# Clears beside the gathers removed, and the gathered rows of two graph layers summed as three bf16 terms

## The chip, the cores and the metric

The kernel runs on one core of one Trainium2 chip. The metric is the device time of one execution in microseconds. The time before is the median of three runs, 2423.22 us (2419.51 to 2429.55). A further execution was profiled: 2415.55 us, of which the profile shows a span of 2413.6 us. All rows below come from that execution.

The engines are named as the profile names them: PE is the matrix engine (PEld its weight loads), DVE the vector engine (VectorE), ACT the scalar engine, POOL GpSimd, SP the engine that issues most of the plain DMAs.

## The reference

A graph has 6250 nodes with 128 features and 106250 edges, sorted by their target node. A normalisation with relu is followed by three layers of mean aggregation, then comes a second normalisation and a message layer:

```
sage(h):  agg[v] = sum over edges (u -> v) of h[u] / max(deg[v], 1)
          out    = agg @ W_l.T + b_l + h @ W_r.T
h  = relu(layernorm(x))
h1 = relu(sage1(h));  h2 = relu(sage2(h1)) + h1;  x = x + sage3(h2)
h  = relu(layernorm(x))
msg[e] = silu(concat(h[src[e]], edge_attr[e]) @ mw1 + mb1)
x = x + h + silu(concat(h, sum of msg over edges into v) @ uw1 + ub1) @ uw2 + ub2
```

What costs time is the sum over incoming edges, four times over. In the kernel these passes are l = 0, 1, 2 (the three aggregations) and l = 3 (the messages).

## The kernel before

The edges are cut into 831 tiles of 128. In pass 0 most edges are handled without a gather. VectorE builds two one-hot tiles for each of the first 600 edge tiles, PE multiplies them into a small table of counts (which source node occurs for which target), ACT moves the tables to a staging tile and sends them to DRAM. SP reads them back in pieces, and a dense product of all node rows with these counts gives the sums. The sum goes in rounds of 49 steps, one step for each 128 source nodes (`dense_step`, line 1128). Passes 1 and 2 read the same tables again: 10 rounds, 490 steps. In these, ACT turns six of seven units of 500 counts from fp16 to a rounded fp32 form and VectorE the seventh (`turn_unit`, line 563), and each step is two products of PE with the high and the low half of the node rows (line 1148).

The remaining edges go in blocks of three tiles. POOL gathers the source rows of a tile from a table in DRAM by an indirect DMA (line 847), three for a block. VectorE makes a one-hot tile of the targets (`hot`, line 1578), PE multiplies rows and one-hot into 31 columns (`sum_block`, line 1098 in passes 1 and 2, line 1101 in pass 0), and VectorE adds these columns to the accumulator (`add`, line 1588). Pass 0 has 117 such blocks, passes 1 and 2 have 77 each. In pass 0 the table holds each row as three bf16 parts, so a block is nine bf16 products and three for the degrees. In passes 1 and 2 it holds fp32 rows, and a block is three fp32 products.

The order of the work is written out by hand in ticks. In passes 1 and 2 a tick is one dense step, and block n stands at tick 34 + n*452//77, about every 5.9 ticks (`block_tick`). In pass 0 a tick is one counted tile, and from tick 78 on a block stands at every 4.4 ticks. Each engine runs its own list in that order. Blocks may be gathered ahead: there are seven places (`LAPS`), and POOL waits until the block that had the place has been summed. In pass 2 the columns of finished nodes are closed chunk by chunk beside the steps (`chunk_work`): average, convolution, second normalisation and message rows, for 13 chunks of 512 nodes.

After each gather of passes 0 to 2 POOL also clears a small tile that nobody reads (line 853). Each such clear waits for the one before it, and 813 gathers have one. Pass 3 gathers 759 tiles by the same line, without clears.

## Time and profile before

| what | us |
|---|---|
| median of three runs | 2423.22 |
| profiled execution, and its span | 2415.55, 2413.6 |
| pass 0, first to last gather | 115.61 to 625.28 |
| pass 1, first to last gather | 690.17 to 997.67 |
| pass 2, first to last gather | 1052.02 to 1362.11 |
| pass 3, first to last gather | 1420.83 to 2397.99 |

The span falls into the four passes with their gathers and three stretches between them, in which the sums are averaged, the layer's small products are made and the table for the next pass is written. The profile's chain of waits tells which engine's work set the end. The groups of instructions show the mean time of one and what ended the idle time before it. In the order of time one sees single instructions with their starts, and in brackets how long the engine had been idle. A matrix product's time overlaps its neighbour's, so its pace is read from one start to the next.

### The profile page before, as it was taken

The numbers are of one execution on the slowest core, as the hardware profiler recorded it, in microseconds if no ns is written. First come the engines' busy times: TensorE is split into PE (matmuls) and PEld (weight loads), VectorE is DVE, ScalarE is ACT, GpSimd is POOL, SyncE is SP. The second block draws the span as 40 slices with busy tenths as digits, with TensorE's granted clock in tenths as the row PEclk, the third lists the DMA queues.
The fourth block names the chain that finished last, engine by engine and source line by source line (L and its number), as shares of the span: only waits on it lengthen the run. The fifth ranks groups of instructions, "written<-read, shape, count | busy, mean of one in ns | idle before, by whom it ended". The sixth has DMA issues, their size and how long they took to land.

```text
span 2413.6 us, 45284 instructions
## 1 busy us (share of the span) xinstructions
PE 2083.5 (86%) x13062; PEld 1628.3 (67%) x13062; DVE 1477.5 (61%) x4334; ACT 1136.1 (47%) x2077; POOL 1845.1 (76%) x2479
## 2 busy tenths in 40 slices
PE   1589988988789888899999959989989898988987
PEld 0234544444367677667777748888889888888876
DVE  8878877777633223354444447666767667676664
ACT  4777766666487666587667732111111111111111
POOL 4488888888478888588888537777777777777775
PEclk9689999999899999999999979999999999999997
DMA  4389888878578777668787644434444444444432
GB/s 121 115 284 302 298 284 263 282 260 279 209 232 254 242 239 233 186 201 260 223 246 240 203 146 136 121 108 121 113 120 114 115 122 112 116 117 117 118 108 54
DMA packets 270049, 447.28 MB, mean 185 GB/s; under 512 B 34149, under 2 KB 219816, under 8 KB 263144
## 3 DMA queue, kind: packets, MB, share of 16 engines
q1 hardware_dynamic: 206680, 267.00, 36.3%
q0 software_dynamic: 55920, 114.62, 17.1%
q10 hardware_dynamic: 7200, 62.72, 6.6%
q8 instruction: 109, 1.79, 0.3%
q14 instruction: 140, 1.14, 0.1%
HBM read 363.79 MB, written 80.42 MB: 184 GB/s over the span
## 4 chain that ended last, share of the span: by engine, by line
POOL 61%; issue 15%; PE 13%; DVE 6%; ACT 2%; DMA 2%; DVEq 0%; POOLq 0%; ACTq 0%; SPq 0%
POOL gath L847 55%; PE bank L1148 7%; POOL early_rest L853 6%; PE bank L1098 2%; DMA gath<-table,src_sb 1%; DMA table<-shared 1%; PE bank L1356 0%; ACT shared L973 0%; DVE acc L1867 0%; PE bank L1218 0%; PE bank L1357 0%; ACT unit L563 0%; DVE iota_f L1374 0%; PE bank L1219 0%; PE bank L1156 0%
## 5 line engine op out<-in xcount | busy, mean ns | idle before, releaser
L847 POOL DMA_INDIRECT gath<-table,src_sb x1572 | 1560.2, 992 | 367.5 <-issue 363.7
L1148 PE MATMUL bank<-unit,halves 128*128 128x500 f32 x1960 | 510.2, 407 | 17.7 <-ACT unit L563 12.3
L563 ACT CAST unit<-region 128x500 fp32r<-128x500 f16 x840 | 454.2, 606 | 124.9 <-PE bank L1148 121.9
L1036 ACT ACTIVATE msg<-msg 128x384 f32<-128x384 f32 x277 | 145.2, 524 | 745.6 <-DVE msg L1676 691.4
L1198 PE MATMUL bank<-source_hot,last_halves 128*128 128x384 f32 x2352 | 494.3, 356 | 0.0
L936 ACT CAST shared<-bank 128x490 f32 x600 | 373.7, 623 | 172.6 <-PE bank L1120 140.2
L1148 PEld LDWEIGHTS bank<-unit,halves 128*128 128x128 f32 x1960 | 362.0, 194 | 93.7 <-ACT unit L563 22.4
L1704 DVE TENSOR_SCALAR source_hot<-source_f,source_col 128x384 fp32r<-128x384 f32 x1176 | 421.0, 421 | 0.8 <-PE bank L1198 0.5
L1198 PEld LDWEIGHTS bank<-source_hot,last_halves 128*128 128x128 f32 x2352 | 414.1, 196 | 3.8 <-issue 3.8
L1588 DVE TENSOR_TENSOR acc<-acc,bank 128x31 f32 (+1 forms) x548 | 104.9, 191 | 398.6 <-PE bank L1098 271.7
L1156 PE MATMUL bank<-region,parts 128*128 128x500 f16 x1176 | 321.6, 381 | 9.8 <-DVE dense_sum L1599 9.8
L1098 PEld LDWEIGHTS bank<-onehot,msg 128*128 128x128 f32 x1662 | 229.5, 200 | 145.2 <-ACT msg L1036 139.0
L1098 PE MATMUL bank<-onehot,msg 128*128 128x31 f32 x1662 | 229.5, 275 | 103.7 <-ACT msg L1036 94.1
L1676 DVE TENSOR_TENSOR msg<-bank,gath 128x384 f32<-128x384 f32 x253 | 140.2, 554 | 260.5 <-issue 183.8
L1633 DVE TENSOR_SCALAR region<-iota_h,key 128x540 bf16<-128x540 f16 x600 | 225.0, 409 | 35.0 <-PE bank L1120 32.2
L1183 PE MATMUL bank<-mw,region 128*128 128x128 f32 x1518 | 238.9, 296 | 1.2 <-DVE shared L1751 1.2
L1117 PE MATMUL bank<-region 128*128 128x490 bf16 x600 | 223.2, 400 | 18.8 <-DVE region L1633 13.0
L1183 PEld LDWEIGHTS bank<-mw,region 128*128 128x128 f32 x1518 | 199.5, 200 | 6.6 <-issue 6.6
L853 POOL MEMSET early_rest<- 128x128 bf16 x813 | 186.1, 229 | 0.4
L1098 PEld LDWEIGHTS bank<-onehot,gath 128*128 128x128 f32 x924 | 123.7, 192 | 55.7 <-issue 47.7
L1156 PEld LDWEIGHTS bank<-region,parts 128*128 128x128 bf16 x1176 | 91.6, 101 | 91.8 <-issue 14.8
L1098 PE MATMUL bank<-onehot,gath 128*128 128x31 f32 x924 | 118.9, 265 | 28.9 <-DMA gath<-table,src_sb 28.4
(165 smaller groups left out, 1763.6 us busy)
## 6 DMA issues: line engine op xcount, KB each, us to landing
region<-counts SPq DMA_DIRECT2D x196, 875.0 KB
counts<-shared ACTq DMA_DIRECT2D x50, 1225.0 KB
region<-in_edge_T SPq DMA_DIRECT2D x138, 384.0 KB, 3.3
gath<-table,src_sb POOLq DMA_INDIRECT x1572
table<-shared SPq DMA_DIRECT2D x36, 256.0 KB, 2.3
table<-parts SPq DMA_DIRECT2D x12, 384.0 KB, 2.6
source_row<-in_src_row SPq DMA_DIRECT2D x24, 192.0 KB, 3.7
acc<-in_x SPq DMA_DIRECT2D x12, 256.0 KB, 5.4
```

The source lines that it names most:

```text
L563: copy(units[h][:, :].rearrange("p (b n) -> p b n", b=RG), ring[:, q, :, h * G:(h + 1) * G]).then_inc(done, 1)
L847: pool.indirect_dma_start(out=(gath if l > 0 else gath_parts)[:, BT * place + j, :], out_offset=None, in_=table[l], in_offset=bass.Indirec ...
L853: nc.gpsimd.memset(early_rest[:, :], 0.0).then_inc(early_rested, 1)
L936: counted = nc.scalar.copy(stage[:, g % 2, :, bass.ds(at, CW)], count_bank(t))
L1098: mm = nc.tensor.matmul(summed_in(l, n)[:, 0:W], of, onehot[:, n % HOTS, j, :], start=(j == 0), stop=(j == BT - 1))
L1117: mm = nc.tensor.matmul(count_bank(t), low_of(t), pairhot[:, t % NPAIR, 0:KW].rearrange("p (h w) -> p h w", h=NTILE), start=True, stop=(t ...
L1148: mm = nc.tensor.matmul(sum_bank(ordinal), halves[:, hi, a, :], units[h][:, :], start=(hi == 0 and a == 0), stop=(hi == NTILE - 1 and a == 1))
L1156: mm = nc.tensor.matmul(sum_bank(ordinal)[:, 0:g * G].rearrange("p (b n) -> p b n", b=g), parts[:, hi, a, :], ring[:, q, 0:g, h * G:(h + 1 ...
L1183: mm = nc.tensor.matmul(edge_bank(n)[:, j * D:(j + 1) * D], efT[:, h % NEF, t * P:(t + 1) * P], mw[:, 1, :], start=True, stop=True)
L1198: mm = nc.tensor.matmul(bank[7][:, 0:BT * P], last_halves[:, h, a, :], source_hot[:, y % NHOT, :], start=(h == 0 and a == 0), stop=False)
L1633: nc.vector.tensor_scalar(pairhot[:, t % NPAIR, :], iota_h[:, :], key[:, t:t + 1], None, ALU.is_equal).then_inc(pairhot_ready, 1)
L1704: nc.vector.tensor_scalar(source_hot[:, y % NHOT, :], source_f[:, k % 2], source_col[:, h:h + 1], None, ALU.is_equal).then_inc(source_hot_ ...
```

## The change

The clears go, with their tile and semaphore. In passes 1 and 2 VectorE now prepares each gathered block: it subtracts from the fp32 rows their own upper 16 bits (read in place as a bf16 number), which gives a rest in fp32, and subtracts from the rest the rest's upper 16 bits, which gives a third term, written as bf16. PE then sums a block by nine bf16 products: the upper halves of the rows and of the rest are read in place with a stride of two, the third term is dense. There are two buffers for rest and third term. The two subtractions stand four ticks ahead of the block in VectorE's list. PE's wait for the gather in passes 1 and 2 becomes a wait for the split, and VectorE waits for the gather. The semaphores of a fallback for leftover edges, which does not run here, are shared by two passes each.

```diff
+SPLIT_AHEAD, NSPLIT = 4, 2
+def splits(l, i):
+    return [n for n in range(BLOCKS[l]) if l in (1, 2) and block_tick(l, n) - SPLIT_AHEAD == i]
...
+        def upper(of):
+            return of.rearrange("p t d -> p (t d)").bitcast(BF16).rearrange("p (t d u) -> p t d u", t=BT, u=2)[:, :, :, 1]
...
                             in_offset=bass.IndirectOffsetOnAxis(ap=src_sb[:, t:t + 1].bitcast(U32), axis=0),
                         ).then_inc(gathered[place], 16)
-                        if l < 3:
-                            after(pool, early_rested, BT * (BLOCKS_BEFORE[l] + n) + j)
-                            nc.gpsimd.memset(early_rest[:, :], 0.0).then_inc(early_rested, 1)
...
-                if l < 3:
+                if l == 0:
                     pe.wait_ge(gathered[place], 16 * BT * (fills + 1))
+                elif l < 3:
+                    pe.wait_ge(block_split, done - BLOCKS_BEFORE[1] + 1)
                 for j in range(BT):
                     t = BT * place + j
-                    if l > 0:
-                        of = msg[:, n % NMSG, j, :] if l == 3 else gath[:, t, :]
+                    if l in (1, 2):
+                        for a, of in enumerate([upper(gath[:, BT * place:BT * (place + 1), :]), upper(rest[:, n % NSPLIT]), third[n % NSPLIT][:, :, :]]):
+                            mm = nc.tensor.matmul(summed_in(l, n)[:, 0:W], of[:, j, :], onehot_h[:, n % HOTS, j, :, 1],
+                                                  start=(j == 0 and a == 0), stop=(j == BT - 1 and a == 2))
+                    elif l > 0:
+                        of = msg[:, n % NMSG, j, :]
                         mm = nc.tensor.matmul(summed_in(l, n)[:, 0:W], of, onehot[:, n % HOTS, j, :], start=(j == 0), stop=(j == BT - 1))
...
+                def split(n):
+                    place, fills = slot(l, n)
+                    g = BLOCKS_BEFORE[l] - BLOCKS_BEFORE[1] + n
+                    of = gath[:, BT * place:BT * (place + 1), :]
+                    dve.wait_ge(gathered[place], 16 * BT * (fills + 1))
+                    after(dve, block_summed, BLOCKS_BEFORE[l] + n - NSPLIT + 1)
+                    nc.vector.tensor_tensor(rest[:, n % NSPLIT], of, upper(of), ALU.subtract).then_inc(rest_made, 1)
+                    dve.wait_ge(rest_made, g + 1)
+                    nc.vector.tensor_tensor(third[n % NSPLIT][:, :, :], rest[:, n % NSPLIT], upper(rest[:, n % NSPLIT]), ALU.subtract).then_inc(block_split, 1)
...
                         if n + HOTS < BLOCKS[l]:
                             hot(n + HOTS)
+                    for n in splits(l, i):
+                        split(n)
                     if l > 0 and (i + TURN_AHEAD) % UNITS == BY_DVE and i + TURN_AHEAD < STEPS[l]:
                         turn_unit(dve, nc.vector.tensor_copy, l, i + TURN_AHEAD, units_by_dve)
```

The added lines move the numbers of the lines behind them: the gathers of line 847 are those of line 866 afterwards, the sums of line 1098 are line 1116, and the dense products of line 1148 are line 1170.

On POOL, at the beginning of pass 0, the list stood before as follows (`acc` is the accumulator that is cleared ahead of the pass, `gath` the seven places, `src_sb` the source numbers):

```order
L773 TENSOR_TENSOR parts<-gath,parts 128x128
L821 MEMSET acc 128x6372
L847 DMA gath<-table,src_sb 128x384
L853 MEMSET early_rest 128x128
L847 DMA gath<-table,src_sb 128x384
```

and now:

```order
L785 TENSOR_TENSOR gath<-acc,parts 128x128
L792 TENSOR_TENSOR parts<-gath,parts 128x128
L840 MEMSET acc 128x6372
L866 DMA gath<-table,src_sb 128x384 x351
L821 TENSOR_LOAD left_flag
```

The 351 gathers of the pass follow each other with nothing between them; passes 1 and 2 have 231 each in the same way.

On VectorE, in pass 1 around the first two blocks, the list stood before as follows (`onehot` is made six blocks ahead, `unit3` is the unit of counts that VectorE turns, `first_row` gives the place in the accumulator):

```order
L1588 TENSOR_TENSOR acc<-acc,bank0 128x31
L1578 TENSOR_TENSOR onehot<-iota_f,rel 128x93
L563 CAST unit3_63<-region_58 128x500
L1584 TENSOR_LOAD first_row
L1584 ISA x2
L1588 ISA
L1588 TENSOR_TENSOR acc<-acc,bank1 128x31
```

and now:

```order
L1600 TENSOR_TENSOR onehot<-iota_f,rel 128x93
L582 CAST unit3_63<-region_58 128x500
L1619 TENSOR_TENSOR rest_75<-gath_57 128x384
L1621 TENSOR_TENSOR third1_77<-rest_75 128x384
L1606 TENSOR_LOAD first_row
L1606 ISA x2
L1610 ISA
L1610 TENSOR_TENSOR acc<-acc,bank1 128x31
```

The two subtractions of block 1, with their wait for its gathers, now stand ahead of the addition of block 1, and behind what was queued for block 0.

On PE, in pass 1 at the first block, the list stood before as follows (`unit` is a unit of counts, `halves` the node rows, two products for a step):

```order
L1148 MATMUL bank<-unit_65,halves 128x500 x2
L1098 MATMUL bank<-onehot,gath 128x31 x3
L1148 MATMUL bank<-unit_66,halves 128x500 x2
L1148 MATMUL bank<-unit_60,halves 128x500 x2
L1148 MATMUL bank<-unit_61,halves 128x500 x2
```

and now:

```order
L1170 MATMUL bank<-unit_65,halves 128x500 x2
L1116 MATMUL bank<-onehot,gath 128x31
L1116 MATMUL bank<-onehot,rest 128x31
L1116 MATMUL bank<-onehot,third_76 128x31
L1170 MATMUL bank<-unit_66,halves 128x500 x2
```

Of the nine products of the block only the first three are shown, the other six repeat them for the second and third tile. The place of the block among the steps is the same.

## Rows read from the trace of the kernel before

**Rows 1.** The page's shares of the chain that ended last, by line.

```profile
POOL gath L847 55%; PE bank L1148 7%; POOL early_rest L853 6%; PE bank L1098 2%; DMA gath<-table,src_sb 1%; DMA table<-shared 1%; PE bank L1356 0%; ACT shared L973 0%; DVE acc L1867 0%; PE bank L1218 0%; PE bank L1357 0%; ACT unit L563 0%; DVE iota_f L1374 0%; PE bank L1219 0%; PE bank L1156 0%
```

**Rows 2.** Passes 0, 1, 2: busy us by engine, then clock, DMA share, GB/s.

```profile
115.00:627.00 512.00, 460.49 (x3735) 233.23 (x3736) 388.80 (x1082) 343.94 (x553) 453.64 (x703) 0.96 0.85 279
690.00:1006.00 316.00, 287.15 (x1427) 235.85 (x1428) 93.83 (x310) 225.14 (x415) 270.59 (x462) 0.97 0.79 245
1052.00:1364.00 312.00, 295.50 (x1509) 240.31 (x1508) 131.63 (x427) 229.29 (x443) 273.18 (x462) 0.98 0.81 251
```

**Rows 3.** POOL in order of time, pass 1, then pass 3: start, us, idle before.

```profile
770.50 0.95 POOL L847 DMA_INDIRECT gath<-table,src_sb  x1 [0.16 <-issue]
...
2049.80 0.94 POOL L847 DMA_INDIRECT gath<-table,src_sb  x1 [0.30 <-issue]
```

**Rows 4.** Groups of pass 0, then pass 1: busy, mean ns of one | idle before.

```profile
L847 POOL DMA_INDIRECT gath<-table,src_sb x351 | 370.3, 1055 | 57.7 <-issue 57.5 <-PE bank L1105 0.2
L853 POOL MEMSET early_rest<- 128x128 bf16 x351 | 84.0, 239 | 0.1
...
L847 POOL DMA_INDIRECT gath<-table,src_sb x231 | 220.1, 953 | 38.7 <-issue 38.2 <-PE bank L1098 0.5
L853 POOL MEMSET early_rest<- 128x128 bf16 x231 | 51.0, 221 | 0.1
```

**Rows 5.** PE's waits for gathers, passes 0, 1, 2: us in total, times, longest.

```profile
PE bank L1101 <- DMA gath<-table,src_sb: 32.4, 23, 5.1
...
PE bank L1098 <- DMA gath<-table,src_sb: 27.3, 31, 2.4
...
PE bank L1098 <- DMA gath<-table,src_sb: 1.1, 3, 0.7
```

**Rows 6.** Pass 0 in time: block 0's last gather, block 0 summed, block 42 summed.

```profile
118.82 0.95 POOL L847 DMA_INDIRECT gath<-table,src_sb  x1 [0.16 <-issue]
...
144.94 0.46 PE L1101 MATMUL bank<-onehot,gath 128*128 128x31 bf16 x9
...
308.31 0.38 PE L1101 MATMUL bank<-onehot,gath 128*128 128x31 bf16 x9 [1.03 <-DMA gath<-table,src_sb]
```

**Rows 7.** Pass 2 in time, a gather that begins inside a VectorE instruction.

```profile
1195.90 0.69 DVE L1757 TENSOR_TENSOR acc<-acc,shared 128x512 f32<-128x512 f32 x1
...
1196.14 1.28 POOL L847 DMA_INDIRECT gath<-table,src_sb  x1 [0.17 <-issue]
```

**Rows 8.** Groups of pass 0: VectorE's long instructions with two inputs in SBUF.

```profile
L1628 DVE TENSOR_TENSOR region<-iota_h,low 128x768 bf16<-128x768 f16 x93 | 88.6, 953 | 14.3 <-PE bank L1120 13.8
L1641 DVE TENSOR_TENSOR region<-iota_f,group_rel 128x500 bf16<-128x500 f32 x94 | 59.5, 672 | 11.5 <-PE bank L1167 10.8 <-issue 0.7
```

**Rows 9.** Groups of the whole span: VectorE's fp32 instructions on SBUF.

```profile
L1757 DVE TENSOR_TENSOR acc<-acc,shared 128x512 f32<-128x512 f32 x12 | 8.2, 685 | 1.3 <-ACT shared L973 1.2
L1510 DVE TENSOR_TENSOR region<-region 128x600 f32<-128x600 f32 x1 | 0.8, 784 | 0.0
L1461 DVE TENSOR_TENSOR region<-region 128x600 f32<-128x600 f32 x1 | 1.6, 1616 | 0.0
```

**Rows 10.** PE in time: a block in pass 0, a block and six steps in pass 1.

```profile
561.02 0.40 PE L1101 MATMUL bank<-onehot,gath 128*128 128x31 bf16 x9
561.26 0.23 PE L1105 MATMUL bank<-onehot,ones_h 128*128 128x31 bf16 x3
...
771.03 0.75 PE L1098 MATMUL bank<-onehot,gath 128*128 128x31 f32 x6
771.62 2.97 PE L1148 MATMUL bank<-unit,halves 128*128 128x500 f32 x12
```

**Rows 11.** The chain, last gather of pass 1; in time, last gather and block of pass 2.

```profile
997.67 4.98 DMA gath<-table,src_sb
...
1362.11 0.95 POOL L847 DMA_INDIRECT gath<-table,src_sb  x1 [0.17 <-issue]
...
1383.18 0.75 PE L1098 MATMUL bank<-onehot,gath 128*128 128x31 f32 x6
```

More of the change, by code:

```diff
@@ L164 @@
 LAPS = 7
-EARLY_REST = 128
 FETCH_EVERY, FETCH_FROM, COPY_AFTER, FETCH_LAG = 11, 4, 12, 16
@@ L399, in gnn_kernel @@
         last_halves = over("last_halves", [P, NTILE, 2, D], F32R, halves_at)
+        rest = over("rest", [P, NSPLIT, BT, D], F32, shared_at + 4 * 4 * 2 * CH)
+        third = [over(f"third{q}", [P, BT, D], BF16, at + 2 * UNIT) for q, at in enumerate([tail_at, key_at])]
+        assert 4 * (4 * 2 * CH + NSPLIT * BT * D) <= 2 * SHARED and len(third) == NSPLIT
+        assert tail_at + 2 * UNIT + 2 * BT * D <= key_at and key_at + 2 * UNIT + 2 * BT * D <= shared_at
+        def upper(of):
+            return of.rearrange("p t d -> p (t d)").bitcast(BF16).rearrange("p (t d u) -> p t d u", t=BT, u=2)[:, :, :, 1]
         stats = sb("stats", [P, 2, JC, 6])
@@ L422, in gnn_kernel @@
         fetch_copied = sem("fetch_copied")
+        rest_made = sem("rest_made")
+        block_split = sem("block_split")
         consts_in = sem("consts_in")
@@ L433, in gnn_kernel @@
         onehot_ready = sem("onehot_ready")
-        early_rest = sb("early_rest", [P, EARLY_REST], BF16)
-        early_rested = sem("early_rested")
         block_summed = sem("block_summed")
@@ L475, in gnn_kernel, with left_from @@
         LEFT = ["idx", "gathered", "onehot", "summed", "added"]
-        lf = [{n: sem(f"left{l}_{n}") for n in LEFT + (["ef_in", "edge_mm", "pre", "msg"] if l == 3 else [])} for l in range(4)]
+        left_sems = [{n: sem(f"left{k}_{n}") for n in LEFT + (["ef_in", "edge_mm", "pre", "msg"] if k == 1 else [])} for k in range(2)]
+        lf = [left_sems[l % 2] for l in range(4)]
+        def left_from(l, each):
+            return l // 2 * each
         def apart(eng):
@@ L639, in left_edges @@
                     with sp.Fori(0, NT) as t:
-                        sp.wait_ge(s["added"], NCH * t + 1)
+                        sp.wait_ge(s["added"], NCH * t + 1 + left_from(l, NCH * NT + 1))
                         apart(sp)
@@ L646, in left_edges @@
                             sp.dma_start(ef_left, edge_T[:, bass.ds(t * P, P)]).then_inc(s["ef_in"], 16)
-                    sp.wait_ge(s["added"], NCH * NT + 1)
+                    sp.wait_ge(s["added"], NCH * NT + 1 + left_from(l, NCH * NT + 1))
             def load_last_rows(c):
@@ L805, in left_edges @@
                     with pool.Fori(0, NT) as t:
-                        pool.wait_ge(s["idx"], 16 * t + 16)
+                        pool.wait_ge(s["idx"], 16 * t + 16 + left_from(l, 16 * NT))
                         apart(pool)
@@ L1268, in left_edges @@
                         else:
-                            pe.wait_ge(s["gathered"], 16 * t + 16)
+                            pe.wait_ge(s["gathered"], 16 * t + 16 + left_from(l, 16 * NT))
                         for c in range(NCH):
                             w = min(CH, NP - c * CH)
-                            pe.wait_ge(s["onehot"], NCH * t + c + 1)
+                            pe.wait_ge(s["onehot"], NCH * t + c + 1 + left_from(l, NCH * NT))
                             if l > 0:
@@ L1281, in left_edges @@
                             mm.then_inc(s["summed"], 1)
-                    pe.wait_ge(s["added"], NCH * NT + 1)
+                    pe.wait_ge(s["added"], NCH * NT + 1 + left_from(l, NCH * NT + 1))
             def update(c):
@@ L1553, in left_edges @@
                             dve.wait_ge(s["edge_mm"], t + 1)
-                            dve.wait_ge(s["gathered"], 16 * t + 16)
+                            dve.wait_ge(s["gathered"], 16 * t + 16 + left_from(l, 16 * NT))
                             nc.vector.tensor_tensor(pre_left, bank[5][:, 0:D], gath_left, ALU.add).then_inc(s["pre"], 1)
@@ L1557, in left_edges @@
                             w = min(CH, NP - c * CH)
-                            dve.wait_ge(s["added"], NCH * t + c + 1)
+                            dve.wait_ge(s["added"], NCH * t + c + 1 + left_from(l, NCH * NT + 1))
                             nc.vector.tensor_scalar(hot_left, iota_h[:, 0:CH], float(CH * c), left[:, bass.ds(t, 1)],
                                                     ALU.add, ALU.is_equal).then_inc(s["onehot"], 1)
-                            dve.wait_ge(s["summed"], NCH * t + c + 1)
+                            dve.wait_ge(s["summed"], NCH * t + c + 1 + left_from(l, NCH * NT))
                             to = acc[:, 0, c * CH:c * CH + w]
@@ L1568, in left_edges @@
                             m.then_inc(s["added"], 1)
-                    dve.wait_ge(s["added"], NCH * NT + 1)
+                    dve.wait_ge(s["added"], NCH * NT + 1 + left_from(l, NCH * NT + 1))
             for l in range(4):
```

## The prediction

> **What bounds the kernel now.** I began with the page's shares of the chain that ended last [rows 1]. The reader is to see that POOL's gathers are 55% of it, and the clears behind them another 6%: the end is set by the pace at which POOL issues gathers, not by PE, though PE is the busiest engine. Then the stretches of the three passes that the change touches [rows 2]. PE is busy for 460 of 512 us in pass 0, 287 of 316 in pass 1 and 295 of 312 in pass 2, so once POOL is quicker, PE is near. VectorE is the engine with room in passes 1 and 2: busy for 94 and 132 us. The DMA engines are busy for 0.85, 0.79 and 0.81 of the time, near full but not full.
>
> Third, POOL's pace. In pass 1 a gather takes 0.95 us and begins 0.16 us after the clear ahead of it; in pass 3, which has no clears, it takes 0.94 and begins 0.30 after the gather ahead of it [rows 3]. By groups, pass 0 has for each of its 351 gathers 1.055 us, 0.164 idle (57.7/351) and a clear of 0.239: 1.458 us. Pass 1 has 0.953, 0.168 and 0.221: 1.342 [rows 4]. Without clears the gap is 0.30, so a clear costs not its 0.22 to 0.24 but 0.09 to 0.10 us.
>
> Fourth, who waits for the gathers. PE waits for them 32.4 us in pass 0, 27.3 in pass 1 and 1.1 in pass 2 [rows 5]. These are caps on what a faster POOL alone can give; in pass 2 PE comes behind POOL for most of the pass.
>
> **Pass 0: the clears go, nothing else changes.** The pace becomes 1.055 + 0.30 = 1.355 us, or 4.07 for a block of three, against 4.37. If POOL set the whole pass, 351 x 0.103 = 36 us would go. But PE has its own pace. Block 0's last gather begins at 118.82 and PE sums the block at 144.94, so POOL has 26 us of lead. By block 42, at 308.31, PE waits for a gather for the first time since [rows 6]. Over these 42 blocks PE needs 163.4/42 = 3.89 us for a block. POOL's new pace eats 0.18 of lead for a block, 21 us over 117 blocks, against a lead of 26 that must still hold the few us from issue to landing. So PE's waits go almost wholly, and PE's own pace is late next. I take 30 of the 32.4 us. Bounds: 0, if two gathers turn out to be no closer in this pass without a clear than with one; and 36.
>
> **Passes 1 and 2: what VectorE adds.** Two subtractions of 384 fp32 elements for each of 154 blocks. A like instruction takes 0.685 us for 512 elements and 0.784 for 600 [rows 9]: 0.0011 us an element, so 0.54 for 384; I take 0.55. One instruction of 600 elements took 1.616 us [rows 9], so an awkward operand could make it 1.03; no row shows the stride of two. A split is 1.1 to 1.2 us with the wait between, and 77 splits add 85 us of busy time to a pass: 179 of 316 in pass 1, 217 of 312 in pass 2. VectorE does not become the bound by its sum.
>
> It costs in a second way. The gather that began at 1196.14, while a VectorE instruction with two inputs in SBUF was running (1195.90 to 1196.59), took 1.28 us where 0.95 is usual: it ended 0.83 us after that instruction [rows 7]. A gather that begins in such an instruction waits for its end. In pass 0 this is the whole excess: 93 instructions of 0.953 us and 94 of 0.672 [rows 8], met at random, would delay a gather by (93 x 0.953² + 94 x 0.672²)/(2 x 512) = 0.124 us on average; 1.055 less pass 1's 0.953, 0.102, is what is there [rows 4]. The two subtractions are of this kind. At random they cost 2 x 0.55²/(2 x 3.9) = 0.078 us for each gather, and with pass 0's ratio of 0.82, 0.064; I take 0.065. Bounds: 0, if they always fall between two starts of gathers; and 1.1/3 = 0.37, if each of the two always catches a gather at its beginning.
>
> The Trainium skill says two things of this in "SBUF — State Buffer", section "Who interferes with whom". A VectorE instruction with two SBUF inputs holds up a GpSimd instruction that reads SBUF, but not one that only writes there. And the generation of descriptors is inferred to need the write side alone, so that a `tensor_tensor` was not seen to stall such a DMA. By the second the delay would be nothing, and POOL could save 15 us more in each of the two passes (231 x 0.065). This trace goes with the first: the gather beside the addition took 1.28 us, and an indirect gather takes its row numbers from SBUF.
>
> **Pass 1, summed.** POOL's pace becomes 0.95 + 0.30 + 0.065 = 1.315 us instead of 1.342: 231 x 0.027 = 6 us. PE's block becomes cheaper: its first product to the next step's first is 0.59 us now (771.03 to 771.62), and nine bf16 products take 0.24 in pass 0 (561.02 to 561.26) [rows 10]. That saves 0.35 us a block, 27 us a pass, with 0 as the lower end if strided weights load as slowly as fp32 ones. In pass 1 it only lengthens PE's wait for POOL, so I count it at nothing. Against it, every block is now ready a split later, which shows once, at the end: 1.2 us. Net 5 us.
>
> **Pass 2, summed.** PE is late here: its last block is summed 21 us after the last gather begins (1362.11 to 1383.18), where in pass 1 the last gather of the chain is followed by 4.98 us until it has landed [rows 11]. So some 15 us can be won from PE's side before POOL is again the bound, and the 27 us of cheaper blocks would pay for it. But in this pass VectorE closes chunks: 132 - 94 = 38 us more of work than in pass 1 [rows 2], some 3 us for each of 13 chunks, in runs. Before, VectorE was ahead of PE with its one-hots by six blocks; a split is ahead by four ticks only. A step is two products, and twelve products take 2.97 us [rows 10], so four ticks are 2 us. A run of 2 to 3 us with a split of 1.2 behind it takes more than that, so PE waits for the split 1 to 2 us, once or twice a chunk: some 15 us. What is queued behind a split, VectorE's own unit of counts and its additions, waits with it. Net: 27 for cheaper blocks, capped at 15 + 6 by POOL, less 15, so 5 us at the most likely. Bounds: 21 (no lumps), and -15 (the lumps are twice as long, and nothing of the cheaper blocks is left).
>
> **The sum.** 30 + 5 + 5 = 40 us, off the profiled execution's 2415.55: 2375.5. That execution lies 7.7 us under the median of the runs, 2423.2, so the time is 2383 as a median. Pass 3 and the stretches between the passes keep their instructions.
>
> **The rivals.**
> - *No delay of gathers, no lumps.* For it speaks that the splits start when a gather lands, which may put them in a steady place between two starts. Against it: four ticks are little, and landing times vary. Pass 0 gives 30, pass 1 231 x 0.092 = 21 less 1.2, pass 2 21: 71 us, 2352. The second of the two statements of the Trainium skill, that such instructions do not hold up descriptors, leads to the same first half of this rival.
> - *VectorE holds PE up in pass 2.* For it: the runs at chunks, against four ticks of cover. Pass 2 loses 15, pass 0 gives 30, pass 1 gives 0: 15 us, 2408.
> - *The clears are not what holds pass 0.* The gap between gathers stays near 0.38 us, or the counts that go out and in by DMA take over as the wait. For it: the DMA share of 0.85 would rise to 0.91. Against it: nothing in pass 0 shows PE waiting for counts. Pass 0 gives 5, the others 10: 2408.
> - *Slower: the splits meet the gathers in step.* Each split starts as the third gather of its block lands, and if that moment lies the same way to POOL's next starts each time, both subtractions catch a gather. A block then costs POOL 3 x 1.25 + 1.1 = 4.85 us instead of 4.03: 63 us more in pass 1, and 63 less the 15 of slack in pass 2. With pass 0's 30 that is 81 us slower, 2504. It decides from the point where a block loses x with 154 x (x - 0.28) - 15 = 30, that is 0.57 us, half of its two subtractions. Against it: landing times would have to be steady.
>
> **How the numbers follow.** The forecast has 0.5, the first rival 0.15, VectorE in pass 2 0.17, the clears 0.10, the slower one 0.08. A measurement of this kernel tells about 0.5%, 12 us, from no change, so the border is 2411. The forecast, whose own range is 2368 to 2400, and the first rival lie under the border; of the two cases at 2408, 0.27 together, rather more than half does, as their sizes may be off by 10 us either way. That makes 0.80 faster, 0.12 the same, 0.08 slower. The range takes in the first rival at its time and the two small ones: 2350 to 2414.
>
> **What would show it.** Right: in pass 0 the gap between gathers is 0.30, PE's waits for gathers there fall under 8 us, and the last gather begins near 595. In passes 1 and 2 gathers have a mean of about 1.01 us, with single ones up to 1.5 beside the subtractions; the subtractions take 0.55 us; nine products take 0.24; pass 1 is still POOL's in the chain, within 10 us of its length before. Wrong: gathers that stay at 0.95 beside the subtractions (the time is then lower), PE waiting for the split for more than 30 us in pass 2, or subtractions of 1 us.

## The result, and the profile after

The changed kernel took 2384.78 us (median of four runs, 2382.45 to 2389.15), the kernel before in the same series 2424.09. The ratio is 0.9839, with a 95% interval of 0.9812 to 0.9866. The profiled execution took 2382.67 us and spans 2380.9. The two profiled executions lie 33 us apart, the medians 39: the profiled one of before was quicker than all the timed ones (2415.55 against 2419.51 to 2429.55), so readings by pass are good to a few us.

The page's chain of waits, shares of the span by engine and line:

```profile
POOL gath L866 36%; PE bank L1178 7%; PE bank L1170 7%; PE bank L1139 4%; DMA gath<-table,src_sb 2%; DVE region L1666 1%; PE bank L1220 1%; PE bank L1120 1%; DVEq L1638 1%; PE bank L1205 1%; DVE dense_sum L1632 1%; PE bank L1123 1%; DVE acc L1647 1%; PE bank L1142 1%; PE bank L1189 1%
```

The gathers held 55% of the chain [rows 1] and now hold 36%; L1178 is the dense product of pass 0, L1170 that of passes 1 and 2, L1139 a count. POOL's part of the chain, clears included, has fallen from 61% to 36%, and PE's has risen from 13% to 27%.

Pass 0, 1 and 2 by windows (length, busy us of PE, PEld, DVE, ACT, POOL, then clock, DMA share, GB/s), against [rows 2]:

```profile
115.00:596.00 481.00, 450.90 (x3708) 230.65 (x3709) 377.74 (x1077) 342.00 (x550) 373.29 (x352) 0.98 0.89 297
663.00:968.00 305.00, 260.17 (x1654) 198.40 (x1653) 173.43 (x461) 222.78 (x411) 227.03 (x231) 0.97 0.81 253
1015.00:1329.00 314.00, 276.86 (x1713) 206.14 (x1714) 202.02 (x568) 229.41 (x443) 227.26 (x231) 0.96 0.79 248
```

PE has 19 us less work in pass 2 and is idle for 37 us of it, where it was idle for 17. In time, the last gather of a pass and the first of the next:

```profile
594.14 0.95 POOL L866 DMA_INDIRECT gath<-table,src_sb  x1 [0.30 <-issue]
...
663.01 1.04 POOL L866 DMA_INDIRECT gath<-table,src_sb  x1 [1.95 <-DMA table<-shared]
...
959.18 0.94 POOL L866 DMA_INDIRECT gath<-table,src_sb  x1 [0.30 <-issue]
...
1015.32 0.97 POOL L866 DMA_INDIRECT gath<-table,src_sb  x1 [1.71 <-issue]
...
1327.21 0.94 POOL L866 DMA_INDIRECT gath<-table,src_sb  x1 [0.30 <-issue]
...
1389.69 0.96 POOL L866 DMA_INDIRECT gath<-table,src_sb  x1 [0.56 <-issue]
```

From these starts comes the measure used below: a pass's length, from its first gather to that of the next pass (the last one to the end of the span). One profiled execution each:

| kernel | pass 0 | pass 1 | pass 2 | pass 3 | median us | ratio, 95% |
|---|---|---|---|---|---|---|
| before | 574.6 | 361.8 | 368.8 | 992.8 | 2424.09 | 1 |
| changed | 547.4 | 352.3 | 374.4 | 991.2 | 2384.78 | 0.9839 |
| e1 clears off, no split | 542.6 | 340.2 | 373.3 | 990.2 | 2361.59 | 0.9768 [0.9755, 0.9781] |
| e2 split, clears kept | 579.0 | 375.5 | 379.4 | 990.9 | 2436.32 | 1.0079 [1.0064, 1.0094] |
| e3 split in pass 1 | 547.5 | 351.3 | 369.1 | 990.9 | 2375.38 | 0.9821 [0.9808, 0.9835] |
| e4 split in pass 2 | 547.2 | 342.1 | 375.4 | 991.6 | 2371.84 | 0.9809 [0.9796, 0.9822] |
| e5 one SBUF input, pass 1 | 548.1 | 344.0 | 375.9 | 989.5 | 2375.91 | 0.9815 [0.9802, 0.9828] |
| e6 cheap blocks, no split | 548.4 | 340.4 | 357.2 | 990.2 | 2353.89 | 0.9724 [0.971, 0.9737] |
| e7 split 8 ticks ahead, pass 2 | 548.8 | 353.1 | 375.7 | 991.7 | 2386.82 | 0.9856 [0.984, 0.9872] |
| e8 two terms, pass 2 alone | 549.0 | 341.6 | 362.8 | 988.0 | 2358.94 | 0.9746 [0.9732, 0.9759] |
| e9 split not waited for, pass 2 | 548.8 | 353.4 | 376.2 | 993.3 | 2387.45 | 0.9862 [0.9838, 0.9885] |
| e10 split not used, pass 2 | 549.5 | 353.6 | 396.4 | 990.0 | 2398.21 | 0.9913 [0.9896, 0.9931] |
| e11 e8, 8 ticks ahead | 548.3 | 342.9 | 362.7 | 990.3 | 2355.84 | 0.9737 [0.9719, 0.9756] |

The experiments ran in three later series, in which the kernel before took 2417.64 us (e1 to e4), 2421.36 (e5 to e8) and 2419.25 (e9 to e11). Each ratio is against the kernel before of its own series; medians of different series differ by that much besides.

So the change gave 27 us in pass 0 and 9.5 in pass 1, and took 5.6 in pass 2. POOL's groups by pass (busy, mean ns of one | idle before, and what ended it), against [rows 4]:

```profile
L866 POOL DMA_INDIRECT gath<-table,src_sb x351 | 372.9, 1062 | 106.8 <-issue 98.3 <-PE bank L1127 8.5
...
L866 POOL DMA_INDIRECT gath<-table,src_sb x231 | 227.0, 983 | 72.0 <-issue 67.3 <-PE bank L1116 2.7 <-DMA table<-shared 1.9
...
L866 POOL DMA_INDIRECT gath<-table,src_sb x231 | 227.3, 984 | 87.3 <-issue 64.8 <-PE bank L1116 22.5
```

Gathers of pass 1 grew from 953 to 983 ns; in pass 2 POOL now waits 22.5 us for PE to free a block (1.0 us before). PE's waits in passes 0, 1 and 2 (us in total, times, longest), against [rows 5]:

```profile
PE bank L1123 <- DMA gath<-table,src_sb: 5.5, 4, 2.3
...
PE bank L1116 <- DVE third L1621: 40.7, 45, 3.1
...
PE bank L1116 <- DVE third L1621: 14.3, 16, 1.9
PE bank L1170 <- ACT unit L582: 13.2, 13, 1.5
PE bank L1240 <- DVE acc L1747: 5.2, 5, 1.7
PE bank L1170 <- DVE unit L582: 3.7, 4, 1.1
```

In pass 1 the wait for the split is the gather's under another name, since the first subtraction waits for the gather in PE's place. The subtractions of pass 1, as groups:

```profile
L1619 DVE TENSOR_TENSOR rest<-gath 128x384 f32<-128x384 f32 x77 | 43.2, 561 | 47.5 <-DMA gath<-table,src_sb 47.1
L1621 DVE TENSOR_TENSOR third<-rest 128x384 bf16<-128x384 f32 x77 | 43.0, 558 | 2.7
```

Lastly the nine products of a block in pass 1, the first and the last of them with the next step:

```profile
845.07 0.18 PE L1116 MATMUL bank<-onehot,gath 128*128 128x31 bf16 x1 [1.68 <-DVE third L1621]
...
845.28 0.18 PE L1116 MATMUL bank<-onehot,third 128*128 128x31 bf16 x1
845.30 4.51 PE L1170 MATMUL bank<-unit,halves 128*128 128x500 f32 x12
```

From 845.07 to 845.30 are 0.23 us, as forecast, against 0.59 for three fp32 products [rows 10].

### The profile page after: what moved, and what is told of

Same layout as the page of the kernel before. It is cut to its first block, busy times and chain, and to the rows that moved or that the text cites. A ratio compares the mean times of both kernels' runs of the same rounds, so it can differ in the third digit from the quotient of the medians.

```text
span 2380.9 us, 45857 instructions
## 1 busy us (share of the span) xinstructions
PE 2026.1 (85%) x13524; PEld 1544.0 (65%) x13524; DVE 1626.5 (68%) x4642; ACT 1136.6 (48%) x2077; POOL 1673.9 (70%) x1666
## 3 DMA queue, kind: packets, MB, share of 16 engines
q1 hardware_dynamic: 206680, 267.00, 36.4%
## 4 chain that ended last, share of the span: by engine, by line
POOL 36%; PE 27%; issue 16%; DVE 12%; DMA 4%; ACT 3%; DVEq 2%; POOLq 0%; ACTq 0%
POOL gath L866 36%; PE bank L1178 7%; PE bank L1170 7%; PE bank L1139 4%; DMA gath<-table,src_sb 2%; DVE region L1666 1%; PE bank L1220 1%; PE bank L1120 1%; DVEq L1638 1%; PE bank L1205 1%; DVE dense_sum L1632 1%; PE bank L1123 1%; DVE acc L1647 1%; PE bank L1142 1%; PE bank L1189 1%
## 5 line engine op out<-in xcount | busy, mean ns | idle before, releaser
L1170 PE MATMUL bank<-unit,halves 128*128 128x500 f32 x1960 | 517.9, 411 | 25.8 <-ACT unit L582 14.4
L1220 PE MATMUL bank<-source_hot,last_halves 128*128 128x384 f32 x2352 | 489.3, 353 | 0.0
L1170 PEld LDWEIGHTS bank<-unit,halves 128*128 128x128 f32 x1960 | 364.9, 196 | 105.8 <-ACT unit L582 24.4
L1178 PE MATMUL bank<-region,parts 128*128 128x500 f16 x1176 | 319.4, 379 | 10.6 <-DVE dense_sum L1632 10.6
L1139 PE MATMUL bank<-region 128*128 128x490 bf16 x600 | 221.0, 396 | 20.3 <-DVE region L1666 13.0
L1666 DVE TENSOR_SCALAR region<-iota_h,key 128x540 bf16<-128x540 f16 x600 | 217.5, 398 | 30.0 <-PE bank L1142 26.7
L1178 PEld LDWEIGHTS bank<-region,parts 128*128 128x128 bf16 x1176 | 91.0, 100 | 91.5 <-issue 13.7
L1600 DVE TENSOR_TENSOR onehot<-iota_f,rel 128x93 f32<-128x93 f32 x548 | 136.6, 251 | 0.4 <-issue 0.2
L1139 PEld LDWEIGHTS bank<-region 128*128 128x128 bf16 x600 | 59.4, 99 | 107.3 <-DVE region L1666 29.1
L1142 PE MATMUL bank<-region 128*128 128x49 bf16 x599 | 128.7, 215 | 0.0
```

The source lines that it names most:

```text
L1139: mm = nc.tensor.matmul(count_bank(t), low_of(t), pairhot[:, t % NPAIR, 0:KW].rearrange("p (h w) -> p h w", h=NTILE), start=True, stop=(t ...
L1142: mm = nc.tensor.matmul(count_bank(t)[:, :, 0:1], low_of(t - 1), pairhot[:, (t - 1) % NPAIR, KW:KEYS].rearrange("p (h o) -> p h o", o=1), ...
L1170: mm = nc.tensor.matmul(sum_bank(ordinal), halves[:, hi, a, :], units[h][:, :], start=(hi == 0 and a == 0), stop=(hi == NTILE - 1 and a == 1))
L1178: mm = nc.tensor.matmul(sum_bank(ordinal)[:, 0:g * G].rearrange("p (b n) -> p b n", b=g), parts[:, hi, a, :], ring[:, q, 0:g, h * G:(h + 1 ...
L1220: mm = nc.tensor.matmul(bank[7][:, 0:BT * P], last_halves[:, h, a, :], source_hot[:, y % NHOT, :], start=(h == 0 and a == 0), stop=False)
L1666: nc.vector.tensor_scalar(pairhot[:, t % NPAIR, :], iota_h[:, :], key[:, t:t + 1], None, ALU.is_equal).then_inc(pairhot_ready, 1)
```

## The experiments

My theory after the result: pass 0's gain is the clears' alone; in pass 1 the split costs half of what the clears give, by delayed gathers; in pass 2 VectorE's subtractions cost more than PE's cheaper blocks give. The rival: the split gains by itself.

### The two halves apart: e1 and e2

e1 is the kernel before without the clear:

```diff
-                            nc.gpsimd.memset(early_rest[:, :], 0.0).then_inc(early_rested, 1)
```

> The clears are taken out of the kernel before, and nothing else: passes 1 and 2 keep their fp32 sums and VectorE splits nothing. My theory: pass 0 gains what it gains in the changed kernel (its first gather to that of pass 1 574.6 us before, 547.4 there, so 27 less here too); pass 1 gains more than with the split, 231 gathers x 0.09 us = 20 us (10 with the split), because no gather is delayed and no block waits for a split; pass 2 gains 0 to 6 us (with the split it lost 6), because PE sets its end and its blocks stay dear. Sum 47 to 53 us: about 2373 us, some 10 us under the changed kernel. The rival theory, that the split pays for itself by cheaper blocks on PE: pass 1 no shorter than with the split, pass 2 longer than with it, about 2395 us.

Measured 2361.59 us, 0.9768 of before, under the changed kernel's interval. Pass 1 fell by 21.6 us, as my theory had it. Pass 2 did not gain as I had thought it might: 373.3 us, 4.5 more than before. POOL stood 26.1 us there for PE to free a block, where it stood 1.0 before the change, so PE set the pace of that pass. Against the kernel before of its own series the gain is 56 us where I expected 47 to 53. Pass 0 gave 5 more than I expected: there this kernel is shorter than every one without clears that was built from the changed kernel (542.6 against 547 to 550). It differs from them there only by the fallback's semaphores and by where tiles lie; this was not tried further. POOL in pass 1:

```profile
L847 POOL DMA_INDIRECT gath<-table,src_sb x231 | 218.5, 946 | 70.8 <-issue 67.8 <-PE bank L1095 3.0
```

e2 is the changed kernel with that line put back.

> The changed kernel with the clears put back behind the gathers of passes 0 to 2; the split and the nine bf16 products stay. My theory: pass 0 as in the kernel before (574.6 us); pass 1 a little longer than before, the pace of 1.337 us plus 0.03 of delay for each of 231 gathers, so 5 to 8 us more; pass 2 5 to 10 us more, since VectorE holds PE up there as it does without clears. Sum 10 to 18 us slower than before: 2434 to 2442. The rival, that the split is a gain by itself (27 us of PE's time in each pass): 10 us or more faster than before, under 2414.

Measured 2436.32 us, 0.8% or 19 us slower than the kernel before in its series, where I expected 10 to 18. The split by itself is a loss, in pass 1 (375.5 us against 361.8, more than I expected) and in pass 2 (379.4 against 368.8). The rival falls.

### One pass at a time: e3 and e4

```diff
-    return [n for n in range(BLOCKS[l]) if l in (1, 2) and block_tick(l, n) - SPLIT_AHEAD == i]
+    return [n for n in range(BLOCKS[l]) if l in (1,) and block_tick(l, n) - SPLIT_AHEAD == i]
```

and PE sums pass 2 as before; e4 has (2,) and pass 1 as before.

> No clears; the split and the bf16 products in pass 1 alone, pass 2 keeps its fp32 sums. My theory: pass 0 27 us shorter than before, pass 1 10 us shorter as in the changed kernel, pass 2 0 to 6 us shorter than before where the changed kernel has 6 more: about 2376 to 2382, a few us under the changed kernel. The rival, that pass 2's 6 us more have nothing to do with VectorE's split there (but with a quicker POOL that leaves PE with its own lag): pass 2 stays 6 us longer than before, and the time is 2385 or more.

> No clears; the split and the bf16 products in pass 2 alone, pass 1 keeps its fp32 sums. My theory: pass 0 27 us shorter than before, pass 1 20 us shorter (gathers of 0.95 us, 1.25 from one to the next), and pass 2 6 us longer than before, as in the changed kernel: about 2375 to 2380. The rival, that without the cheaper blocks PE holds pass 1 up: pass 1 10 us shorter or less, with PE's waits for gathers gone, and the time 2385 or more.

Measured 2375.38 and 2371.84 us. The passes do what they do in the changed kernel, each by itself: pass 1 is 351.3 us with the split and 342.1 without, pass 2 is 375.4 with it and 369.1 without. The same pass 2, without a split, took 373.3 in e1, so a single length of this pass is good to some 4 us from one build to the next. By medians each pass does better without its split, but the two intervals overlap with the changed kernel's; what stands clear of it is e1, without either.

### Pass 1, the delayed gathers: e5

```diff
-nc.vector.tensor_tensor(rest[:, n % NSPLIT], of, upper(of), ALU.subtract).then_inc(rest_made, 1)
+nc.vector.tensor_tensor(flat(rest[:, n % NSPLIT]), other, flat(of), ALU.subtract).then_inc(rest_made, 1)
```

with `other = bank[7][:, 0:BT * D]`, and the second subtraction likewise, in pass 1 alone.

> The changed kernel, but in pass 1 alone each of the two subtractions takes one operand from a bank of PSUM instead of SBUF (so the sums of that pass are not the reference's; what PE, POOL and VectorE execute is the same in number and size). Theory 1: what the split costs in pass 1 is the delay of the gathers that begin beside an instruction with two inputs in SBUF. Then the gathers of pass 1 fall from a mean of 0.983 us to the 0.946 that they take without a split, 231 x 0.037 = 8.5 us go, pass 1 is 343 to 345 us instead of 352, the time 2374 to 2378 us. Theory 2, that the split costs pass 1 by its own length between gather and sum: pass 1 stays at 352 us, the time at 2385.

Measured 2375.91 us, pass 1 344.0 us. POOL's and VectorE's groups in that pass:

```profile
L866 POOL DMA_INDIRECT gath<-table,src_sb x231 | 218.2, 945 | 70.9 <-issue 69.2 <-PE bank L1116 0.9 <-DMA table<-shared 0.8
```

```profile
L1622 DVE TENSOR_TENSOR rest<-bank,gath 128x384 f32<-128x384 f32 x76 | 42.2, 555 | 36.0 <-DMA gath<-table,src_sb 35.5
L1627 DVE TENSOR_TENSOR third<-bank,rest 128x384 bf16<-128x384 f32 x75 | 41.8, 558 | 2.6
```

The subtractions take the same 0.56 us, in the same number, at the same places, and the gathers are back at 945 ns. They still meet: 66 gathers begin inside a subtraction, and these take 0.944 us on average. The edit also replaces a read with a stride of two by a dense one, but the addition of [rows 7], which held a gather, read densely too. Theory 1 holds: 8.3 of the 12 us by which pass 1 with the split is longer than without (352.3 against 340.2) are the delay of gathers by instructions with two inputs in SBUF. The other 3.8 us (344.0 against 340.2) I put down to the split's own length, the one between the last gather and its sum among it. That is argued, and its size is uncertain: pass 1 without a split took from 340.2 to 342.9 us in the five experiments that have it so (e1, e4, e6, e8, e11), which leaves 1 to 4 us.

### Pass 2, what the blocks give and what the split takes: e6, e9, e10

e6 has no subtractions, and PE multiplies the upper halves three times:

```diff
-for a, of in enumerate([upper(gath[...]), upper(rest[:, n % NSPLIT]), third[n % NSPLIT][:, :, :]]):
+for a, of in enumerate([upper(gath[...])] * 3):
```

> No clears and no subtractions; PE sums a block of passes 1 and 2 by nine bf16 products, all of the upper halves of the gathered rows (so the sums are not the reference's), and waits for the gather. It shows what the cheaper blocks are worth when VectorE has nothing to do for them. Theory 1: pass 2 is PE's, and the split on VectorE takes back what the cheaper blocks give. Then pass 1 is as without a split, 340 to 342 us, and pass 2 falls from 369 to 375 us to about 352, where POOL is the bound again (231 gathers x 1.25 us = 289 us, and the 61 us from the last gather to the next pass); the time is 2337 to 2345 us. Theory 2, that pass 2 is held by something that neither the blocks nor the split touch: pass 2 stays at 369 us or more, the time at 2358 or more.

Measured 2353.89 us: 357.2 us in pass 2, between the two theories and nearer the first. The cheaper blocks are worth 12 us there (369.1 in e3) to 16 (373.3 in e1), and in pass 1 nothing (340.4 against 340.2). The window of pass 2 in e3, then in e6, and PE's waits in e6:

```profile
1014.00:1324.00 310.00, 294.67 (x1498) 241.30 (x1498) 130.70 (x426) 229.02 (x443) 220.51 (x231) 0.97 0.80 251
```

```profile
1004.00:1303.00 299.00, 274.57 (x1717) 205.81 (x1718) 132.01 (x427) 228.97 (x443) 219.78 (x231) 0.96 0.83 262
```

```profile
PE bank L1170 <- ACT unit L582: 15.0, 15, 1.9
PE bank L1240 <- DVE acc L1747: 5.5, 5, 1.7
PE bank L1170 <- DVE unit L582: 2.0, 4, 1.1
```

e9 has all the subtractions and the cheap products of e6 in pass 2, and PE waits for the gather there, not for the split:

```diff
-                if l == 0:
+                if l in (0, 2):
                     pe.wait_ge(gathered[place], 16 * BT * (fills + 1))
```

The edit also makes POOL wait, before it gathers into a place, until VectorE has split the block that had the place; POOL stood 3.4 us for that in pass 2.

> The changed kernel, but in pass 2 PE does not use what VectorE splits: it waits for the gather and sums nine bf16 products of the upper halves (so that pass's sums are not the reference's). VectorE makes all its subtractions as before. Theory 1: in pass 2 the subtractions cost by the time that they take from VectorE's other work, for which PE waits (units, freed accumulators), and not by PE's own wait for the split. Then pass 2 stays at 370 to 376 us (374.4 in the changed kernel), the time at 2380 to 2387 us. Theory 2: it is PE's own wait for the split. Then pass 2 falls towards the 357 us that it takes with cheap blocks and no subtractions, and the time to 2366 to 2372.

Measured 2387.45 us, pass 2 376.2: theory 1. PE never waits for a split, and the pass is as long as with the wait. PE's waits in it, then its window:

```profile
PE bank L1172 <- ACT unit L582: 18.8, 15, 3.1
PE bank L1172 <- DVE unit L582: 13.6, 10, 2.3
PE bank L1242 <- DVE acc L1749: 6.4, 5, 1.7
```

```profile
1018.00:1333.00 315.00, 275.13 (x1710) 205.12 (x1709) 201.84 (x567) 228.24 (x442) 227.26 (x231) 0.96 0.79 246
```

Against e6 PE has the same 275 us of work, VectorE 70 more, and PE is idle for 40 us instead of 24: the waits for units and for the closed chunk (L1749) have grown from 22.5 to 38.8. How a subtraction gets there is seen in time, in e9:

```profile
1071.64 0.59 DVE L1621 TENSOR_TENSOR rest<-gath 128x384 f32<-128x384 f32 x1 [1.18 <-DMA gath<-table,src_sb]
...
1072.26 0.56 DVE L1623 TENSOR_TENSOR third<-rest 128x384 bf16<-128x384 f32 x1
...
1074.24 0.26 DVE L1649 TENSOR_TENSOR acc<-acc,dense_sum 128x100 f32 x1 [0.87 <-DVE acc L1649]
...
1075.62 0.67 DVE L582 CAST unit<-region 128x500 fp32r<-128x500 f16 x1
1076.34 0.75 PEld L1172 LDWEIGHTS bank<-unit,halves 128*128 128x128 f32 x4 [2.73 <-DVE unit L582]
1076.34 1.18 PE L1172 MATMUL bank<-unit,halves 128*128 128x500 f32 x4 [2.30 <-DVE unit L582]
```

VectorE runs its list in order. It stands 1.18 us for a gather that the split needs, splits for 1.2, does the additions that were due (with 0.87 and 0.84 us of waiting for one another), and only then turns the unit for which PE has been standing 2.30 us. Behind the pass's first gather there are nine such waits for VectorE's unit. A split stands among VectorE's last nine instructions ahead of each of them, and a wait for a gather ahead of two. In the whole of the pass VectorE is busy for 202 of 315 us: it is not full, it is late.

A rival is left in part. The subtractions delay gathers in pass 2 too (0.984 us in e9, 0.951 in e6, 7.6 us over 231 gathers), and no run takes that delay away there. But POOL stood 20.5 us for PE in e9's pass 2, PE stood only 1.0 us for a gather and VectorE 5.8, so at most some 7 us of the loss can come by that way.

e10 lets PE sum fp32 rows in pass 2 while VectorE splits for nobody. POOL waits for the splits as in e9, 5.2 us in all:

> The changed kernel, but in pass 2 PE sums the gathered fp32 rows by three fp32 products as before the change, and waits for the gather; VectorE makes all its subtractions all the same and nobody uses them there. Compared with the kernel that splits in pass 1 alone (2375.4 us, pass 2 369.1 us), it adds the subtractions to pass 2 and nothing else. Theory 1, that they cost by VectorE's other work: pass 2 grows by 10 to 18 us to 379 to 387, the time to 2385 to 2394 us. Theory 2, that they cost only where PE waits for them: pass 2 stays at 369 to 373 us, the time at 2375 to 2380.

Measured 2398.21 us: longer, as theory 1 has it, and by more than I gave it. Pass 2 is 396.4 us in the profiled execution, which lies 8.7 us above the median of its runs; by medians, 2398.21 less e3's 2375.38, the subtractions cost some 23 us. Its pass 2 in one window:

```profile
1015.00:1353.00 338.00, 308.31 (x1496) 250.12 (x1496) 204.92 (x575) 231.85 (x448) 228.74 (x233) 0.93 0.74 230
```

PE's granted clock was 0.93 there, against 0.97 in e3 and 0.95 or more in the other windows of pass 2. PE is busy for 13.6 us more than in e3 (308.31 against 294.67) and idle for 14.4 more (29.7 against 15.3). So in this execution only half of the growth is waiting; the other half is slower products, and no run shows whether the subtractions bring the lower clock about. With e6 the count is: subtractions cost pass 2 17 to 19 us where blocks are cheap (374.4 and 376.2 against 357.2), some 23 where they are not, a figure in which the clock may have a part; cheap blocks give back 12 to 16.

### Place or amount: e7, e8, e11

e7 moves the split ahead in pass 2:

```diff
-SPLIT_AHEAD, NSPLIT = 4, 2
+SPLIT_AHEAD, NSPLIT = {1: 4, 2: 8}, 2
```

> The changed kernel with the split of pass 2 eight ticks ahead of its block in VectorE's list instead of four; nothing else. Theory 1: it is the short cover of four ticks that lets VectorE's runs at the chunks hold PE up. Then PE's waits for the third term in pass 2 fall from 14.3 us to under 5, and pass 2 from 374 us to 360 to 368: 2370 to 2379 us. Theory 2: with two buffers the earlier split only waits itself, for the sum of the block before last, and with it what stands behind it on VectorE; or it is the amount of VectorE's work in a run and not its place. Then pass 2 stays within 3 us of 374, or is longer: 2382 to 2395 us.

Measured 2386.82 us, pass 2 375.7: theory 2. PE's waits in that pass:

```profile
PE bank L1170 <- ACT unit L582: 15.6, 15, 2.2
PE bank L1240 <- DVE acc L1747: 10.6, 6, 2.7
PE bank L1170 <- DVE unit L582: 9.9, 10, 2.1
PE bank L1116 <- DVE third L1621: 0.9, 1, 0.9
```

The wait for the split is gone, 14.3 to 0.9 us, and the other three have grown from 22.1 to 36.1. In sum the four were 36.4 us and are 37.0. VectorE itself now stands 8.8 us for gathers that a split needs, where it stood 2.6: an earlier place in its list is also an earlier wait, and what is behind it waits with it.

e8 halves the amount, in pass 2 alone:

```diff
-nc.vector.tensor_tensor(rest[:, n % NSPLIT], of, upper(of), ALU.subtract).then_inc(rest_made, 1)
-dve.wait_ge(rest_made, g + 1)
-nc.vector.tensor_tensor(third[n % NSPLIT][:, :, :], rest[:, n % NSPLIT], upper(rest[:, n % NSPLIT]), ALU.subtract).then_inc(block_split, 1)
+nc.vector.tensor_tensor(third[n % NSPLIT][:, :, :], of, upper(of), ALU.subtract).then_inc(block_split, 1)
```

> No clears; pass 1 keeps its fp32 sums; in pass 2 VectorE makes one subtraction, written as bf16, and PE sums a block by six bf16 products, upper halves and rest rounded to bf16 (the third term is left out). Against the kernel that has the full split in pass 2 alone (2371.8 us, pass 2 375.4 us), VectorE's added work is halved, 85 to 43 us, PE's block 0.25 to about 0.17 us, and a split is ready 0.6 us earlier. Theory 1, that VectorE's work sets what the split costs: pass 2 falls to 360 to 367 us, the time to 2357 to 2364, the level of the kernel without any split. Theory 2, that any wait of PE for VectorE costs as much: pass 2 stays at 373 or more, the time at 2369 or more.

> The kernel with one subtraction and six bf16 products in pass 2 alone (2358.9 us, pass 2 362.8 us), its subtraction eight ticks ahead instead of four. Theory 1, that the place of the subtraction only moves the waits from the split to what stands behind it on VectorE: pass 2 stays within 3 us of 362.8, the time at 2356 to 2362 us. Theory 2, that with one short subtraction there is room to hide it and PE's 7.4 us of waiting for it go: pass 2 is 355 to 359 us, the time 2350 to 2355.

Measured 2358.94 and 2355.84 us; pass 2 takes 362.8 and 362.7. With none, one and two subtractions a block, pass 2 takes 357.2, 362.8 and 374.4 us: the amount decides more than the place. The steps are not for subtractions alone, since e8's blocks are six products and not nine, and PE is busy there for 3.4 us less than in e6 (271.18 against 274.57); so one subtraction a block costs the pass 6 to 9 us, and two cost 17. Eight ticks in e11 change nothing beyond the intervals, again: PE's wait for the split falls from 7.4 to 0.5 us, VectorE's for gathers grows from 8.1 to 14.7, and PE's for VectorE's units from 3.3 to 9.7. Both kernels beat the changed one by about 1%. Against e1, which keeps the full fp32 sums, the ratios are 0.2 and 0.3% lower with intervals that touch: e1 is the plain version that beats both the kernel before and the changed one, and two terms may buy a little more for a less exact sum.

## Why the prediction was right, and where not

The forecast was 40 us less, 2383; 39 less by medians, 2384.78. The terms fared differently, and that the total came so near is partly luck. By passes the profiled executions gained 27.2 and 9.5 us and lost 5.6, 31 us in sum where I had 40: the misses of passes 1 and 2 (4.5 too few, 10.6 too many) cancel in part, and the medians happen to lie 6 us further apart than the two profiled executions.

**Pass 0: right.** The gap is 0.30 us, PE's waits for gathers fell from 32.4 to 5.5, the last gather begins at 594.14 where I had written 595. The last gather came 31.1 us earlier, the pass is 27.2 shorter. That the clears cost 0.09 and not their 0.24 us, and that PE's pace would be next, were the two readings that made it; e1 shows that the clears alone do it, so the rival by which they do not hold pass 0 falls.

**Pass 1: right in kind, two sizes off in opposite ways.** I had 5 us, it is 9.5. The gathers were delayed by 0.030 us against before, not by 0.065. The step that failed is the formula that lets a gather wait for the whole rest of a subtraction. Over the timeline of pass 1, 67 of 231 gathers begin inside one, which is just what chance gives (154 x 0.56 / 296 = 29%), so they do not meet in step, as the slower rival had it. But these 67 take 1.069 us on average and the other 164 take 0.947: 67 x 0.122 = 8.2 us. That they are held at all is what the first rival denied; e5 shows it. The rows show why it is so little:

```profile
824.56 0.56 DVE L1621 TENSOR_TENSOR third<-rest 128x384 bf16<-128x384 f32 x1
824.65 1.28 POOL L866 DMA_INDIRECT gath<-table,src_sb  x1 [0.30 <-issue]
...
828.44 0.56 DVE L1619 TENSOR_TENSOR rest<-gath 128x384 f32<-128x384 f32 x1 [1.33 <-DMA gath<-table,src_sb]
828.74 1.08 POOL L866 DMA_INDIRECT gath<-table,src_sb  x1 [0.30 <-issue]
...
835.47 0.61 DVE L1619 TENSOR_TENSOR rest<-gath 128x384 f32<-128x384 f32 x1 [1.34 <-DMA gath<-table,src_sb]
835.49 0.94 POOL L866 DMA_INDIRECT gath<-table,src_sb  x1 [0.30 <-issue]
```

The first two gathers end 0.81 and 0.82 us after the subtraction, as the one of [rows 7] did by 0.83. In all, 44 of the 67 do so: they begin 0.04 to 0.42 us after a subtraction's start and end 0.81 to 0.82 after its end. Alone a gather takes 0.945, so the first 0.13 us or so of the overlap are free: the delay is what is left of the subtraction less 0.13. And the six gathers that begin within 0.022 us of a subtraction's start, as the last one, are not held at all. I had the 0.83 in hand and did not subtract it. By e1 the clears alone are worth 21.6 us in this pass, as the 231 x 0.092 of the first rival had it; the split takes 12 of it back, where I had 15 for the gathers and 1.2 for the end. By e5 what is left for the end is 1 to 4.

**Pass 2: wrong in sign, by two sizes and by the wait.** I had 5 us less, it is 5.6 more. Cheaper blocks gave 12 to 16 us and not the 21 up to POOL's pace: PE's busy time fell by 20 us (294.67 to 274.57 from e3 to e6) and not 27, and part of that came back as waits for ACT's and VectorE's units and the closed chunk (14.1 us in e3, 22.5 in e6), for PE is not alone in its pace. The subtractions took 17 and not 15. The step that failed is more than a size: I had priced the four ticks of cover, with PE waiting for the split. e7 and e9 take that wait away, by place and by not waiting, and the pass stays. The sentence that was worth the price is the one that I left without one: what is queued behind a split waits with it. The rival of VectorE holding PE up in pass 2 was thus the better description of that pass, though its 15 us were too many and its pass 1 too poor.

**What I said would show it wrong.** PE waits for the split 14.3 us in pass 2, under the 30 that I had named, the subtractions take 0.56, and gathers do not stay at 0.95: by these signs the forecast stood, while the pass grew. Of the signs for it, the mean of the gathers came short (0.983 us in pass 1, not 1.01), and so did the longest of them (1.34, not 1.5). A sign on one wait does not see a loss that is spread over three others.

PE's granted clock does not explain pass 2: it is 0.96 in e6, e9 and the changed kernel alike, and PE is busy for 274.57, 275.13 and 276.86 us there, so nearly all that pass 2 has over e6 is PE's idle time. Open: how much of it comes by the delayed gathers (at most some 7 us, by e9); why the clock was 0.93 in e10; and the 5 us of pass 0 by which e1 is better than all that were built from the changed kernel.

## What to carry to other kernels

Test the halves of a double change apart: here one half was worth more than the whole. An operation put on an engine that has room costs what stands behind it in that engine's order, not its share of busy time; removing the wait that the profile names for it only renames the loss, as e7 did, so vary the amount of work before its place. A short filler between long instructions on an engine can cost less than its length (here 0.09 to 0.10 us for a clear of 0.22 to 0.24); read the gap with and without it.

## What the runs showed of the hardware

A VectorE subtraction with one operand in PSUM and one in SBUF takes the same time as with both in SBUF (555 against 561 ns) and delays no indirect gather (the mean of the pass is 945 ns against 983; the 66 that begin inside such a subtraction take 944). A VectorE subtraction that reads one operand with a stride of two takes no longer either (561 and 558 ns against 555 and 558 dense). PE reads its weights with a stride of two bf16 at no loss that shows; weight loads in the changed kernel's pass 2, minimum, median and maximum in ns:

```profile
L1116 PEld LDWEIGHTS bank<-onehot,gath x216: 96/97/151, 1031.4 to 1326.4; 128*128 128x128 bf16 x108
...
L1116 PEld LDWEIGHTS bank<-onehot,third x216: 95/96/106, 1031.4 to 1326.4; 128*128 128x128 bf16 x108
```

The strided one (gath) has a median of 97 ns, the dense one (third) 96.
